# Graph attention with residual and LayerNorm: ScalarE's second high part of the coming quad's input, moved from the middle of one round to the end of the round before

## The reference

```
q = x @ Wq.T; k = x @ Wk.T; v = x @ Wv.T + bv            # split into 12 heads
a = einsum(q, k) * 384**-0.5 + adj[:, None]              # adj is the bias of the scores
a = where(all(a == 0, axis=-1), -inf, a); a = nan_to_num(softmax(a))
out = layernorm(x + (einsum(a, v) @ Wo.T + bo))
```

## Time and profile before

| | us |
|---|---|
| median of 3 runs (lowest, highest) | 1248.02 (1247.92, 1248.37) |
| time of the profiled execution | 1248.19 |
| its span, first to last instruction | 1246.4 |

### The profile page before, as it was taken

The page is one execution under the profiler, slowest core; times in us unless marked ns, Lnnn a source line. Parts: engine busy times, 40 slices in busy tenths (PEclk is TensorE's granted clock), DMA queues, the critical chain, the costliest instruction groups (busy, mean ns, idle before and its releaser), DMA issues.

```text
span 1246.4 us, 34374 instructions
## 1 busy us (share of the span) xinstructions
PE 1218.8 (98%) x11796; PEld 1057.3 (85%) x11796; DVE 1054.4 (85%) x5094; ACT 1017.0 (82%) x4007; POOL 866.7 (70%) x775
## 2 busy tenths in 40 slices
PE   8999999999999999999999999999999999999996
PEld 7888888888888888888888888888888888888885
DVE  5788888888888888888888888888888888888986
ACT  6888888888888878888887888788888888887874
POOL 1777777677677777777776777677777767776774
PEclk9999999999999999999999999999999999999999
DMA  6022211222121222112221212221122212122100
GB/s 232 22 72 86 79 55 54 82 75 80 56 77 61 72 86 80 54 54 83 74 79 61 80 55 71 86 79 54 58 83 71 80 62 79 54 71 86 54 28 26
DMA packets 58895, 88.85 MB, mean 71 GB/s; under 512 B 3680, under 2 KB 54624, under 8 KB 58720
## 3 DMA queue, kind: packets, MB, share of 16 engines
q1 hardware_dynamic: 58720, 86.65, 21.4%
HBM read 61.47 MB, written 25.17 MB: 70 GB/s over the span
## 4 chain that ended last, share of the span: by engine, by line
PE 77%; ACT 19%; DVE 2%; issue 1%; POOL 1%; DMA 0%; POOLq 0%; SPq 0%; DVEq 0%
PE turn_bank L208 17%; PE turn_bank L210 17%; PE turn_bank L209 17%; PE pT_bank L256 12%; ACT probs L496 11%; PE score_bank L244 9%; PE turn_bank L268 6%; ACT pT L503 4%; ACT qkT L484 2%; ACT xT_hi L472 1%; DVE neg_a L624 0%; DVE out_sb L688 0%; DMA xT_raw<-xT_dram 0%; POOL inv_std L779 0%; POOL probs L772 0%
## 5 line engine op out<-in xcount | busy, mean ns | idle before, releaser
L496 ACT ACTIVATE probs<-neg_a,neg_max 128x128 f32<-128x128 f32 x1536 | 596.1, 397 | 3.7 <-DVE neg_max L624 3.5
L772 POOL TENSOR_TENSOR probs<-probs,row_scale 128x768 f32<-128x768 f32 x256 | 376.7, 1471 | 199.8 <-DVE row_scale L652 199.8
L765 POOL TENSOR_TENSOR fold<-neg_a 128x384 f32<-128x384 f32 x256 | 282.9, 1105 | 124.5 <-DVE neg_max L624 124.4
L624 DVE CUSTOM_DVE_ANT_0 neg_a<-score_bank,adj_sb 128x128 f32<-128x128 f32 x1536 | 333.4, 287 | 0.1
L503 ACT ACTIVATE pT<-pT_bank 128x384 f32<-128x384 f32 x512 | 220.7, 484 | 102.9 <-PE pT_bank L256 102.8
L496 ACT ACTIVATION_READ_ACCUMULATOR probs<-neg_a,neg_max 128x1 f32 x1536 | 302.5, 197 | 0.0
L208 PE MATMUL turn_bank<-xT_hi,w_hi 128*128 128x512 f32 (+1 forms) x594 | 240.9, 406 | 2.3 <-DVE w_lo L606 2.3
L210 PE MATMUL turn_bank<-xT_hi,w_lo 128*128 128x512 f32 (+1 forms) x594 | 231.7, 390 | 0.0
L209 PE MATMUL turn_bank<-xT_lo,w_hi 128*128 128x512 f32 (+1 forms) x594 | 230.6, 388 | 0.0
L256 PE MATMUL pT_bank<-ident,probs 128*128 128x128 f32 x1536 | 217.1, 278 | 0.3 <-ACT pT L503 0.3
L256 PEld LDWEIGHTS pT_bank<-ident,probs 128*128 128x128 f32 x1536 | 173.8, 141 | 21.1 <-issue 1.1
(11 more groups left out here) (39 smaller groups left out, 1961.9 us busy)
## 6 DMA issues: line engine op xcount, KB each, us to landing
xT_raw<-xT_dram SPq DMA_DIRECT2D x32, 768.0 KB, 4.7
x_sb<-x_dram SPq DMA_DIRECT2D x32, 768.0 KB, 4.7
out_dram<-out_sb SPq DMA_DIRECT2D x128, 192.0 KB, 1.9
adj_sb<-adj_dram SPq DMA_DIRECT2D x32, 256.0 KB, 3.2
w_raw<-wq_t_dram SPq DMA_DIRECT2D x1, 576.0 KB, 5.7
w_raw<-wk_t_dram SPq DMA_DIRECT2D x1, 576.0 KB, 6.8
w_raw<-wv_t_dram SPq DMA_DIRECT2D x1, 576.0 KB, 7.8
w_raw<-wo_t_dram SPq DMA_DIRECT2D x1, 576.0 KB, 8.4
```

The costliest lines, as they stand in the source:

```text
L496: last = nc.scalar.activation(probs[t % 2][:, u, :], neg_a[t % 2][:, u, :], ACT.Exp, bias=neg_max[t % 2][:, u:u + 1], scale=-1.0, accum_ou ...
L624: last = nc.vector.tensor_tensor_reduce(out=neg_a[t % 2][:, u, :], in0=score_bank[trio][:, c * N:(c + 1) * N], in1=adj_sb[q % 2][:, b, :], ...
L765: nc.gpsimd.tensor_tensor(fold[:, u, :], neg_a[t % 2][:, u, 0:N // 2], neg_a[t % 2][:, u, N // 2:N], ALU.add).then_inc(fold_done, 1)
L772: nc.gpsimd.tensor_tensor(probs[t % 2][:, u, :], probs[t % 2][:, u, :], row_scale[:, u].unsqueeze(2).broadcast_to([P, HALF, N]), ALU.mult) ...
```

## The change

ScalarE makes part 1 of `xT_hi` of quad q+2 at the end of round 0, right behind part 0, and no longer in the middle of round 1, between the second `keep_qk` and the third trio of exponentials. Parts 0 and 2 stay where they are. This holds for the quads with q + 2 < 32, which are 30. Nothing is added or removed on any engine, and the instructions of TensorE, VectorE, GpSimd and SyncE stand in the order they had.

```
@@ -536,8 +536,6 @@
                 if t == TAIL + 5:
                     keep_qk(LAST, 4, turn)
-                if b == 1 and has_after:
-                    keep_xT_hi(q + 2, 1)
                 if more2:
                     exp_trio(t + 2, 2)
@@ -548,6 +546,7 @@
                 if b == 0 and has_after:
                     act.wait_ge(v_psum, t + 4)
                     keep_xT_hi(q + 2, 0)
+                    keep_xT_hi(q + 2, 1)
                 if b == 1 and not tail:
                     keep_qk(q + 1, 5, turn)
```

## The result

| | before | after |
|---|---|---|
| median, us (lowest, highest) | 1247.92 (1247.74, 1249.89), 7 runs | 1243.27 (1242.15, 1244.38), 7 runs |
| profiled execution, its span | 1248.19, 1246.4 | 1242.15, 1240.4 |
| quad period, scores to scores at the start of round 2 | 38.03 | 37.82 |

The ratio is 0.9958 (95% interval 0.9948 to 0.9969): faster. The forecast was 1242.2 us in a range of 1238.8 to 1246.0.

The account below looks back on a forecast made before the run. ScalarE was taken to bound the kernel through the scores' wait for `qkT` in round 2; 29 x 0.19 + 0.30 = 5.8 us off 1248.19 gives 1242.4, stated as 1242.2 us, range 1238.8 to 1246.0.

Parts of the forecast that it names:

- The bottleneck: ScalarE, 19% of the chain, bounds the kernel where round 2's scores wait for the last `qkT` copy.
- 0.30 us per quad from starts: Scores at the start of round 2 begin 1.09 us after the attention, unheld 0.79; the loss is 0.30 us a quad.
- Part one: Copy leaves round 1: last `keep_qk` starts at 626.14, held by TensorE; the scores' wait goes entirely, 0.30 us per quad.
- Part two, cost 0: Copy enters the end of round 0: its 0.52 us fits in 1.03 us of ScalarE idle time, costing nothing.
- The rival in which ScalarE is late: Second copy stretches at the end of round 0, delaying `oT_hi` and VectorE down to `keep_v`; slower, up to 1257 us; chance 0.05.
- What is late next: Round 2's second v projection waits for VectorE's `keep_v`, losing 0.11 us a quad and leaving 0.19 us.
- The rival in which this wait does not bind: VectorE's round 2 begins 0.1 us earlier, so `keep_v` holds nothing; 9.0 us come back, 1239.0 us; chance 0.20.
- The last quad: The last of 30 quads, followed by the tail's graphs with another v projection order, keeps its 0.30 us.
- The sum: 29 x 0.19 + 0.30 = 5.8 us gained over all quads.
- More lost in round 2: VectorE or ScalarE later by 0.1 to 0.2 us, for example through the exponentials; 1245 to 1248 us; chance 0.17.
- The time: Whole kernel: 1242.4 us from the profiled execution's 1248.19, stated as 1242.2 us for the median.

Follow-up runs that it names:

- 1536-column copy: Changed kernel plus an unused ScalarE copy of 3 x 512 columns behind the two high parts at the end of round 0: 1251.22 us, ratio 1.0023.
- versions with the late fold: Changed kernel with `keep_v` ahead of part 2 of `xT_lo` and GpSimd's second fold of round 2 behind scaling and `inv_std`: 1241.24 us, again 1240.52 us.
- repeated changed kernel: The changed kernel measured again with no edit: 1243.91 us, ratio 0.9965 to the kernel before.
- Two of the experiments: Changed kernel with VectorE's round 2 `keep_v` between the third and fourth bias trios, 1244.55 and 1244.99 us; with it ahead of `xT_lo` part 2, 1254.59 us.

## Why the prediction was right

**The bottleneck.** Right: the wait of the scores for ScalarE's last copy was what ScalarE's 19% of the chain cost, and it went.

**0.30 us per quad from starts.** Right, and it is the whole of what this wait could return in a quad. With both waits gone the period is 37.73, 0.30 less than before.

**Part one.** `keep_qk` begins when the product allows it, 0.43 us after its start, and the scores are not held.

**Part two, cost 0.** Right: 0.49 us of idle time is left. The rival in which ScalarE is late didn't occur by itself. The 1536-column copy shows that its mechanism is real and that its price is lower: the prediction handed all the lateness of `oT_hi` on to the v projection, and of 0.43 us only 0.24 arrived.

**What is late next.** Right: `keep_v`, released by nothing earlier on VectorE. I took 0.11 us, and 0.09 is what it is. The rival in which this wait does not bind is refuted by the 0.92 us in the changed kernel and by the versions with the late fold, which show what its absence brings: 0.09 us of the period, and 2.7 to 3.4 us by their medians against that of the repeated changed kernel, which comes from another set.

**The last quad.** Wrong: I let it keep its 0.30 us. TensorE in the round behind it waits for a later `keep_v` in front of an attention; first before, then after:

```profile
1167.43 0.86 PE L268 MATMUL turn_bank<-pT,v_sb 128*32 128x128 f32 x24 [0.77 <-DVE v_sb L613]
```

```profile
1161.52 0.86 PE L268 MATMUL turn_bank<-pT,v_sb 128*32 128x128 f32 x24 [0.96 <-DVE v_sb L612]
```

Between the scores of that round and the next ones there were 8.67 us before and are 8.94 now, so 0.27 of its 0.30 us was given back.

**Two quads gain nothing.** The prediction found no further wait behind `keep_v`. In two of the 29 periods there is one. They were 38.01 us both before and are 38.00 and 37.97 in the changed kernel, where all others are 37.82. In the two, VectorE stands idle for 0.27 us in front of `y_sb`, and the profile names no engine that it waits for. The same idle piece is there before the change. The first q projection comes 0.71 us behind this `y_sb`, so now the wait for it ends last:

```profile
176.12 0.56 DVE L668 TENSOR_TENSOR y_sb<-turn_bank,x_sb 128x384 f32<-128x384 f32 x1 [0.27 <-issue]
...
781.42 0.56 DVE L668 TENSOR_TENSOR y_sb<-turn_bank,x_sb 128x384 f32<-128x384 f32 x1 [0.27 <-issue]
```

```profile
176.83 0.47 PE L208 MATMUL turn_bank<-xT_hi,w_hi 128*128 128x512 f32 x1
```

What makes VectorE idle there is not known.

**The sum.** That it comes out at 5.8 us is luck in part. The smaller loss at `keep_v` adds 0.6 us to the forecast, the two quads take 0.4 from it and the last quad 0.3. In the profiles the last scores begin at 1219.08 before and at 1213.16 after, 5.9 us earlier, and 0.1 us of that was there before the first quad that the change touches.

**More lost in round 2.** Refuted for 27 of the 29 periods; the two above are cases of it, by `y_sb` and not by the exponentials. Two of the experiments are cases too: a small change of order on VectorE brought 0.05 us of extra loss in the one and 0.38 in the other.

**The time.** The medians differ by 4.7 us, in the repeated set too, while the profiled executions differ by 6.0. The profiled execution of the changed kernel was the fastest of its seven. So the forecast of 1242.2 met the profile, and the median lies 1.1 us above it; of that difference the runs show only what the last section tells.

## What to carry to other kernels

A wait of an engine that is busy 98% is measured from start to start against the same pair of instructions where nothing holds them, and the gain of removing it ends at the next wait behind it. Look for that one on the engine that the change does not speed up, and add its instruction's start to the measured hand-over time. While this next wait stands, the formerly late engine may even be a little late again at no cost (an extra step of 0.3 us here), and once it is gone the same lateness costs its full length. Before instructions of VectorE and GpSimd are reordered, see which of the two begins first.

## What the runs showed of the hardware

**VectorE and GpSimd.** Whichever of the two began first made the other wait. `xT_lo` first: 0.69 us, fold 1.40. Fold first by 0.30 us: fold 1.01, `xT_lo` 1.25. That agrees with the Trainium skill (GPSIMD Engine Reference, Specifications), by whose table the SBUF interfaces are shared with VectorE and instructions with two SBUF inputs contend. In the rows the later one does most of its work behind the end of the earlier: `xT_lo` ends 0.54 us after the fold, and the fold 0.88 us after `xT_lo`. It is so for a tiny instruction too: `live` on 6 columns took 0.40 us in place of 0.17 and ended at 631.01, the fold beside it at 630.99.

**The end of the program.** Two executions of the changed kernel stand at the same point at 1213 us and end 1.9 us apart. The stretch of 1229 to 1237 us (columns: us, then busy time and count of PE, PEld, DVE, ACT and POOL, granted clock, DMA share, GB/s), first in the first profile, then in the second:

```profile
1229.00:1237.00 8.00, 3.69 (x41) 2.85 (x39) 4.51 (x10) 1.36 (x3) 1.60 (x3) 1.00 0.07 25
```

```profile
1229.00:1237.00 8.00, 5.53 (x45) 4.63 (x43) 3.06 (x6) 1.36 (x3) 1.59 (x3) 0.79 0.07 25
```

The granted clock of TensorE was 1.00 in the one and 0.79 in the other, mixed from the levels of 2.4 and 1.2 GHz. The last output projection shows what that costs, its first and its last matmul in the first profile and then in the second:

```profile
1233.32 0.45 PE L208 MATMUL turn_bank<-w_hi,oT_hi 128*128 128x384 f32 x1 [1.75 <-DVE oT_lo L660]
...
1234.82 0.34 PE L210 MATMUL turn_bank<-w_hi,oT_lo 128*128 128x384 f32 x1
```

```profile
1233.88 0.69 PE L208 MATMUL turn_bank<-w_hi,oT_hi 128*128 128x384 f32 x1 [1.75 <-DVE oT_lo L660]
...
1236.60 0.51 PE L210 MATMUL turn_bank<-w_hi,oT_lo 128*128 128x384 f32 x1
```

From the first to the last it is 1.50 us in the one and 2.72 us in the other, which is 1.2 of the 1.9 us. TensorE had waited 1.75 us for `oT_lo` before it in both. By then the two were 0.56 us apart already; that part was not followed further. The output projection at 1220 us ran at the lower level in both (0.32 us from start to start for 0.17), in the second profile from its first matmul and in the first from its fifth. What decides between the two levels is open. That the other runs of the changed kernel spread over 2 us for the same reason is not shown.
